# Graph layer on one core: one row tile instead of three masked while h is made, and no row sums in that stage

## The reference

```
h      = max(layernorm(x), 0)                 # layernorm over the 256 columns, no affine part
mask   = (adj > 0)
deg    = sum(mask, axis=1)
agg    = (mask @ h) / max(deg, 1)
self_f = h @ W_self + b_self
nb_f   = agg @ W_nb + b_nb
out    = x + relu(concat(self_f, nb_f) @ W_comb + b_comb)
```

## Time and profile before

| what | value |
|---|---|
| median of three runs | 1092.21 us |
| the profiled execution, its own time | 1092.21 us |
| its span, first to last instruction | 1089.9 us (2.3 us lie around it) |
| TensorE busy | 1019.8 us, 94% |
| VectorE busy | 675.9 us, 62% |
| ScalarE busy | 585.3 us, 54% |
| mean granted TensorE clock | 0.973 |
| DMA | 295.03 MB, mean 271 GB/s |

### The profile page before, as it was taken

The page is one execution under the profiler, slowest core; times in us unless marked ns, Lnnn a source line. Parts: engine busy times, 40 slices in busy tenths (PEclk is TensorE's granted clock), DMA queues, the critical chain, the costliest instruction groups (busy, mean ns, idle before and its releaser), DMA issues.

```text
span 1089.9 us, 14154 instructions
## 1 busy us (share of the span) xinstructions
PE 1019.8 (94%) x4704; PEld 467.1 (43%) x4704; DVE 675.9 (62%) x1111; ACT 585.3 (54%) x681; POOL 57.3 (5%) x57
## 2 busy tenths in 40 slices
PE   6666667899999999999999999999999999999998
PEld 4232233444444444444444444444444444444443
DVE  4555665478866666666666666666666666666621
ACT  4544455467755555555555555555555555555510
POOL 1022222400000000000000000000000000000000
PEclk9878888999999999999999999999999999999999
DMA  9622221079998888888888888888888888888700
GB/s 355 267 78 77 78 77 44 1 303 409 419 369 320 322 318 321 323 318 325 326 322 323 320 322 319 323 324 319 321 330 319 321 320 319 324 321 321 283 21 10
DMA packets 59377, 295.03 MB, mean 271 GB/s; under 512 B 7008, under 2 KB 24544, under 8 KB 26592
## 3 DMA queue, kind: packets, MB, share of 16 engines
q1 hardware_dynamic: 59360, 294.81, 72.8%
HBM read 286.39 MB, written 8.39 MB: 270 GB/s over the span
## 4 chain that ended last, share of the span: by engine, by line
PE 87%; DVE 7%; issue 2%; POOL 2%; ACT 1%; DMA 0%; SPq 0%; POOLq 0%
PE pair_ps L389 41%; PE sum_ps L389 39%; PE pair_ps L380 7%; DVE x_again L489 2%; DVE x_again L482 2%; DVE mask L469 1%; POOL x_again L273 1%; DVE mask_t L495 1%; ACT z L308 1%; PE pair_ps L410 1%; DVE x_again L485 1%; DMA z<-in_L_gnn_W_nb_dram 0%; DVE z L501 0%; POOL x_again L270 0%; PE pair_ps L404 0%
## 5 line engine op out<-in xcount | busy, mean ns | idle before, releaser
L318 ACT ACTIVATE mask<-mask 128x2048 uint8<-128x2048 uint8 x256 | 488.0, 1906 | 344.1 <-DVE mask_t L475 343.9
L389 PE MATMUL sum_ps<-z,mask_t 128*128 128x512 f16 x2048 | 448.8, 379 | 1.0 <-DVE z L501 1.0
L389 PE MATMUL pair_ps<-z,mask_t 128*128 128x512 f16 x2048 | 445.1, 379 | 0.0
L475 DVE STREAM_TRANSPOSE mask_t<-mask 128x512 uint32<-128x512 uint32 x256 | 181.6, 710 | 241.5 <-PE pair_ps L389 121.5
L469 DVE TENSOR_SCALAR mask<-stage 128x2048 uint8<-128x2048 int32 x256 | 307.3, 1200 | 3.7 <-DMA stage<-in_adj_dram 3.7
L389 PEld LDWEIGHTS pair_ps<-z,mask_t 128*128 128x128 fp8e4 x2048 | 197.9, 98 | 237.7
L389 PEld LDWEIGHTS sum_ps<-z,mask_t 128*128 128x128 fp8e4 x2048 | 198.2, 98 | 234.8 <-DVE z L501 1.5
L380 PE MATMUL pair_ps<-mask_t 128*128 128x512 f16 x384 | 110.0, 447 | 53.3 <-DVE mask_t L495 53.3
L380 PEld LDWEIGHTS pair_ps<-mask_t 128*128 128x128 f16 x384 | 41.3, 111 | 114.0 <-DVE mask_t L495 58.6
L313 ACT ACTIVATE self_f<-pair_ps 128x512 f32<-128x512 f32 x32 | 19.1, 597 | 102.3 <-PE pair_ps L380 102.3
L501 DVE SCALAR_TENSOR_TENSOR z<-pair_ps,z 128x512 f16<-128x512 f32 x32 | 21.9, 684 | 69.2 <-ACT z L308 69.2
(11 more groups left out here) (38 smaller groups left out, 173.1 us busy)
## 6 DMA issues: line engine op xcount, KB each, us to landing
stage<-in_adj_dram SPq DMA_DIRECT2D x256, 1024.0 KB, 5.8
self_f<-in_x_dram SPq DMA_DIRECT2D x16, 512.0 KB, 17.3
x_again<-in_x_dram SPq DMA_DIRECT2D x64, 128.0 KB, 5.3
out_dram<-x_again SPq DMA_DIRECT2D x64, 128.0 KB, 5.1
z<-in_L_gnn_W_comb_dram SPq DMA_DIRECT2D x1, 512.0 KB, 4.2
z<-in_L_gnn_W_self_dram SPq DMA_DIRECT2D x1, 256.0 KB, 2.9
z<-in_L_gnn_W_nb_dram SPq DMA_DIRECT2D x1, 256.0 KB, 4.4
z<-in_L_gnn_b_comb_dram SPq DMA_DIRECT2D x1, 128.0 KB, 6.1
```

The source lines that it names most:

```text
L318: act.activation(mask[:, a, :], mask[:, a, :], ACT.Copy, accum_out=deg_part[:, n, a:a + 1]).then_inc(counted, 1)
L389: mm = pe.matmul(acc[n], bytes_of[:, :, s], z16[:, SUB * e + s, :], start=(e == 0 and s == 0), stop=(e == CHUNKS - 1 and s == SUB - 1))
L475: dve.transpose(mask_t[:, n, :, a, :], src).then_inc(transposed, 1)
```

## The change

EARLY_TILES becomes 1. In the first stage VectorE masks and transposes only the four groups of row tile 0 (j = 1, 3, 5, 7), and ScalarE counts only these. The eight groups of row tiles 1 and 2 are masked, transposed and counted after the loop, in tile order, ahead of row tile 3. early_units() goes, and TensorE makes no unit of sums within the loop; row tiles 0 and 1 are summed after it, each in one piece, as row tiles 2 and 3 already are. SyncE issues the loads in the same order of tiles.

```diff
-EARLY_TILES = 3
+EARLY_TILES = 1
 EARLY_GROUPS = EARLY_TILES * QUAD
...
-def early_units():
...
@@ SyncE
-            for r in range(1, EARLY_TILES):
-                load_tile(r)
-
...
             for r in range(EARLY_TILES, 8):
                 load_tile(r)
                 if r - 3 >= XRING:
                     sp.wait_ge(stored, (r - 6) * DONE)
-                x_tile(r - 3)
+                if r >= 3:
+                    x_tile(r - 3)
@@ ScalarE, after the loop
-            for a in range(QUAD):
-                count(EARLY_TILES, EARLY_TILES, a)
+            for r in range(EARLY_TILES, SUB):
+                for a in range(QUAD):
+                    count(r, r, a)
@@ TensorE, in the loop over j
-                for r, e in UNITS[j]:
-                    if e == 0:
-                        pe.wait_ge(transposed, (r + 1) * QUAD)
-                        if r == 1:
-                            pe.wait_ge(c_ready, 1)
-                    pe.wait_ge(z_low, 2 * (e + 1))
-                    sum_chunk(r, e)
                 if j >= 1:
                     project(j - 1)
@@ TensorE, after the loop
-            for r in range(2):
-                for e in LEFT[r]:
-                    if e == 0:
-                        pe.wait_ge(transposed, (r + 1) * QUAD)
-                        pe.wait_ge(c_ready, 1)
-                    pe.wait_ge(z_low, 2 * (e + 1))
-                    mm = sum_chunk(r, e)
-                mm.then_inc(main_done, 1)
-
             pe.wait_ge(self_copied, PAIRS)
             pe.wait_ge(z_low, PAIRS)
...
+            tile(0, 0)
+            tile(1, 1)
             tile(2, 2, (0, 1))
             tile(3, 3, (2,))
@@ VectorE, after the loop
             dve.wait_ge(fold_ready, QUAD)
-            form_mask(3, 0)
-            turn_mask(3, 3, 0)
-            spread_counts(0, 0)
-            spread_counts(1, 1)
-            for a in range(1, QUAD):
-                form_mask(3, a)
-                turn_mask(3, 3, a)
-            spread_counts(2, 2)
-
+            for r in range(EARLY_TILES, SUB):
+                for a in range(QUAD):
+                    form_mask(r, a)
+                    turn_mask(r, r, a)
+                spread_counts(r - 1, r - 1)
```

More of the change, by code:

```diff
@@ L71, in graph_layer @@
     last = TILES - 1
-    UNITS, LEFT = early_units()
     with ExitStack() as ctx:
```

## The result

The changed kernel takes 1100.46 us, the median of four runs (1098.73 to 1101.25), against 1092.3 us before. The ratio is 1.0072, 95% interval 1.0055 to 1.0090: slower, by about 8 us. That is under 1%, but clear of the spread between runs. The forecast was 1100.6 us in a range of 1093.5 to 1104.0.

The account below looks back on a forecast made before the run. The prediction took a five-engine chain to bound the first stage and TensorE's sums the second. Terms of -14.9, -3.5, +19.9 and +6.9 summed to +8.4 us on 1092.21, giving 1100.6 us, range 1093.5 to 1104.0.

Parts of the forecast that it names:

- The masks: First stage's chain: eight mask groups leave, each worth 1.86 us, for a gain of 14.9 us.
- TensorE's clock: First stage: ten projects on the chain lengthen from 43.1 to 50.0 us at a lower clock, a loss of 6.9 us.
- The stage's end: End of the first stage: four units of sums leave TensorE's chain, for a gain of 3.5 us.
- The units that come back: Second stage: 23 units of sums are made there instead, at 0.865 us each, for a loss of 19.9 us.
- The second stage is fed: Second stage: masks and loads of row tiles 1 to 3 arrive in time, so TensorE never waits; price nothing.
- Rival D: Second stage starves: a slow first load makes row tile 2's last mask 1.4 us late; 1102.0 us or more, chance 0.04.
- C: First stage: TensorE's clock stays up and the ten projects take 2.78 us each; -13.8 us, 1078.4 us, chance 0.07.
- B: First stage: projects stay as long as before, so no clock loss; +1.5 us, 1093.7 us, chance 0.11.
- E: First stage: something else takes the masks' place, so its chain isn't shortened; +16.4 us, 1108.6 us, chance 0.03.
- part 4: First stage: the forecast's term for projects lengthened by TensorE's lower clock, +6.9 us.

Follow-up runs that it names:

- sums_off: The kernel before with no sums by TensorE in the first stage, masks of row tiles 0 to 2 left in it: 1113.08 us, ratio 1.0199.
- mask_slot: The kernel before with each mask and transpose ahead of low_of_z instead of behind it, and ScalarE's count ahead of copy_self: 1060.66 us, ratio 0.9713.
- fill12: The changed kernel with 12 unused matmuls ahead of the project in each even step from 10 to 28: 1077.95 us, ratio 0.9874.
- before_fill: The kernel before, all masks and sums in place, with 12 unused matmuls ahead of the project in each even step from 10 to 28: 1078.38 us, ratio 0.9885.
- tile0_units: The changed kernel with the sum units of row tile 0 back in the first stage's loop: 1093.62 us, ratio 1.0019.
- late_masks: tile0_units with row tile 1's four masks put in the first stage's last steps, 29 to 32: 1087.32 us, ratio 0.9964.

## Why the prediction was right

**The masks.** Predicted 1.86 us each and 7.93 us for a cycle without one; the changed kernel has 7.93 in its cycles. sums_off has 9.78 with the masks and no sums, so the price does not hang on what TensorE does. mask_slot adds what the trace of before already told and the prediction did not draw on: the price is one of place. Moved away or moved by one step, a mask is gone from the chain alike.

**TensorE's clock.** This was the term with the widest bounds, 44.6 to 53.2 us for the ten projects. 50.0 was taken, from the three projects that ran ahead of any sum; 50.25 was measured. That the two agree to 0.25 us is luck beside the spread of the single ones, 4.19 to 5.32, and the four runs of the kernel lie 2.5 us apart. Luck lies in the choice of rows too: the three had waits of 2.96, 2.96 and 5.09 us ahead of them, the ten had 3.26 and then 4.06 to 4.49. That TensorE's pauses make the projects long is shown by fill12 and before_fill, where matmuls were put into them. That the sums' leaving lengthens them is shown by sums_off, 5.2 of the 7.1 us; the other 2 us came with the masks' leaving and are not explained. The wait just ahead of a project does not give its length: in sums_off it is 5.1 us in most cycles and the ten sum to 48.3, less than the 50.25 of the changed kernel with its shorter waits. What decides where between 2.76 and 5.3 us a project falls stays open. The two rules of the Trainium skill that were weighed (TensorE: Matmul & The Clock Gate) come out so. "What's actually happening" puts the slow start at under 1% of a typical span and advises against fitting a count of slow matmuls. The 7.1 us are 0.6% of this span, so the size agrees; but leaving them at nothing would have given 1093.7, as they are most of the 8 us between the two kernels. "Loop structure matters more than you think" has a wait for DMA of 8 us before each matmul as its example, where the waits here are for VectorE and about half as long; with every burst slow it would have given 1103.8. Six of the ten were slow to the end, so the trace lies nearer to this one.

**The stage's end.** -2.9 us instead of -3.5: four units did go, but the first turn there ran at the slow clock, 0.85 us instead of the 0.45 of rows 4, which is most of the difference.

**The units that come back.** +19.7 us measured for 19.9, with no wait in the second stage.

**The second stage is fed.** Row tile 1 was masked 8.5 us after the stage's end (9 forecast), row tile 2 at 18 us (18 forecast), row tile 3 at 28. That there was a margin at all is due to row tile 0 being summed in one piece; tile0_units, which takes that piece away, lost 9.3 us in this place. Rival D had the right mechanism but looked for it in the loads; the masks of row tile 1 are the nearer danger.

**The rivals.** C, the clock that stays up, was priced at 1078.4 and did not happen; fill12, which makes it happen, gave 1077.95. B and E are answered by the ledger. (The forecast's price for E, +16.4, leaves part 4 out; with it E would be 1115.5.) None of the steps failed; what the forecast could not know from the trace of before was where within its bounds the clock term would fall.

## What to carry to other kernels

Work that fills the waits of an engine has to be weighed against what feeds it on the chain, piece by piece. Here the eight masks were worth 14.9 us, and the 23 units were worth 19.9 less 3.5 at the stage's end and 7.1 of TensorE's clock, so taking both away lost. The two did not have to go together: 15 of the 23 units belong to row tile 0, whose masks stayed, and late_masks, which keeps these and moves the masks, is at 1087.32 us. Before a step is moved to another stage, look for a wait on its own engine, within the same cycle, that is long enough to hold it: the masks cost nothing one place earlier, ahead of a wait of 4.5 us. And where TensorE's bursts lie on the chain with a few microseconds of idle time between them, price them at both of its clocks, and try matmuls without a use in the gap.

## What the runs showed of the hardware

Extra matmuls made the kernel faster: ten times 12 matmuls that nobody reads, some 26 us of added TensorE work, took 22.5 us off the time, since the projects, now behind a wait of 1.9 us or less, all ran at 2.76 us, and those of the changed kernel, behind mostly 4.1 to 4.5 us, at 4.2 to 5.3. Between the two the wait does not decide: after 2.75 us both a fast and a slower project were seen.

A VectorE instruction on four columns took 2.30 us when GpSimd's addition on 1024 columns (2.34 us) had started 0.06 us ahead of it, and 0.16 us otherwise; a mask took 2.39 instead of 1.22 beside the same addition, while the low halves of h and z, which read PSUM, ran at their usual 0.68 us. One wait that lets the short instruction go first took most of 23 us off the time. The Trainium skill, SBUF — State Buffer, "SBUF: two separate sides", states that VectorE and GpSimd share one pair of ports as an exclusive lock, held for the whole instruction by whichever starts first, where the VectorE instruction has two inputs in SBUF or runs in a 2-port mode. The runs agree for the short instruction, which has two, and for the low halves, which have one. The mask has one as well; that it runs in a 2-port mode is not shown here.
